# A cross-attention and mixture-of-experts kernel: how router logits are turned and added, and which engine normalises the first tile of a pair

## What is computed

```python
def xattn(q, k, v, mask, Wq, Wk, Wv, bq, bk, bv):
    qp = relu(q @ Wq + bq); kp = relu(k @ Wk + bk); vp = relu(v @ Wv + bv)
    logits = relu(qp @ kp.T) / sqrt(512) + mask
    return relu(logits @ vp)
def ffn(x, gate_w, Wu, Wv, Wo):
    topv, topi = top_k(x @ gate_w, 2)
    w = softmax(topv)
    Y = (silu(x @ Wu[e]) * (x @ Wv[e])) @ Wo[e]      # for each expert e
    return sum over the 2 chosen experts of w * Y
x = x + xattn(layernorm(x), ctx, ctx, ...)
x = x + ffn(layernorm(x), ...)
```

## Time and profile before

| | us |
|---|---|
| median of 3 runs | 447.36 |
| lowest, highest | 447.08, 450.7 |
| the profiled execution | 448.53 |
| its span, first to last instruction | 446.8 |

### The profile page before, as it was taken

The page is one execution under the profiler, slowest core; times in us unless marked ns, Lnnn a source line. Parts: engine busy times, 40 slices in busy tenths (PEclk is TensorE's granted clock), DMA queues, the critical chain, the costliest instruction groups (busy, mean ns, idle before and its releaser), DMA issues.

```text
span 446.8 us, 10794 instructions
## 1 busy us (share of the span) xinstructions
PE 422.6 (95%) x3206; PEld 377.5 (84%) x3206; DVE 345.6 (77%) x1102; ACT 275.0 (62%) x602; POOL 187.1 (42%) x214
## 2 busy tenths in 40 slices
PE   8999999999999999979898899999999899999990
PEld 6588998888889988878787689999998799999980
DVE  1779899999999999998778877766667577666661
ACT  1677777877877778767575566676754344444430
POOL 2001245555556556653467523333331533333341
PEclk9999999999999999999999999999999999999997
DMA  8713235755555655535758598999547999999500
GB/s 291 239 61 95 93 107 180 256 187 175 192 192 191 189 176 169 188 118 174 280 190 294 175 299 262 325 331 331 162 114 225 328 364 333 346 301 274 211 2 0
DMA packets 51800, 94.06 MB, mean 211 GB/s; under 512 B 7585, under 2 KB 18337, under 8 KB 51745
## 3 DMA queue, kind: packets, MB, share of 16 engines
q1 hardware_dynamic: 40384, 59.28, 42.3%
q0 software_dynamic: 11360, 34.09, 20.0%
HBM read 52.04 MB, written 44.97 MB: 217 GB/s over the span
## 4 chain that ended last, share of the span: by engine, by line
PE 54%; DVE 23%; ACT 6%; issue 6%; DMA 4%; SPq 3%; POOL 1%; POOLq 0%; DVEq 0%; ACTq 0%
PE psQ L1292 9%; PE psQ L1294 9%; PE psQ L1293 9%; PE psT L1288 6%; DVE st L916 4%; DVE x L905 3%; PE psS L1292 2%; DVE qpT L805 2%; PE psO L1292 2%; PE psQ L1288 2%; PE psO L1294 2%; PE psO L1293 2%; PE psZ L1292 2%; PE psZ L1294 2%; PE psZ L1293 2%
## 5 line engine op out<-in xcount | busy, mean ns | idle before, releaser
L805 DVE TENSOR_TENSOR qT<-psT,qT 128x512 fp32r<-128x512 f32 x110 | 74.3, 689 | 33.8 <-ACT qT L613 33.5
L1292 PE MATMUL psQ<-wuv,qT 128*128 x312 | 95.0, 304 | 0.0
L1293 PE MATMUL psQ<-wuv,qT 128*128 x312 | 88.4, 283 | 0.0
L1294 PE MATMUL psQ<-wuv,qT 128*128 x312 | 88.1, 282 | 0.0
L541 POOL DMA_INDIRECT z_dram<-zb x64 | 71.0, 1109 | 31.5 <-issue 15.2
L1292 PE MATMUL psQ<-qT,wq 128*128 128x256 f32 x256 | 75.3, 294 | 0.0
L613 ACT ACTIVATE qT<-psT 128x512 fp32r<-128x512 f32 x110 | 63.6, 594 | 18.0 <-PE psT L1288 18.0
L1294 PE MATMUL psQ<-qT,wq 128*128 128x256 f32 x256 | 72.5, 283 | 0.0
L1293 PE MATMUL psQ<-qT,wq 128*128 128x256 f32 x256 | 72.5, 283 | 0.0
L1292 PEld LDWEIGHTS psQ<-wuv,qT 128*128 128x128 f32 x312 | 59.2, 190 | 4.4
L1293 PEld LDWEIGHTS psQ<-wuv,qT 128*128 128x128 f32 x312 | 59.5, 191 | 0.0
(11 more groups left out here) (225 smaller groups left out, 1056.5 us busy)
## 6 DMA issues: line engine op xcount, KB each, us to landing
wq<-z_dram SPq DMA_DIRECT2D x46, 264.0 KB, 4.0
xin<-in_x_dram SPq DMA_DIRECT2D x11, 512.0 KB, 3.6
z_dram<-spare SPq DMA_DIRECT2D x18, 264.0 KB, 3.6
qpT<-z_dram SPq DMA_DIRECT2D x18, 264.0 KB, 4.0
xn<-z_dram SPq DMA_DIRECT2D x14, 264.0 KB, 3.1
xin<-acc_dram SPq DMA_DIRECT2D x13, 256.0 KB, 4.4
zT_ctxT<-acc_dram SPq DMA_DIRECT2D x12, 256.0 KB, 4.6
zT_ctxT<-in_x_dram SPq DMA_DIRECT2D x5, 512.0 KB, 3.4
```

The source lines that it names most:

```text
L805: nc.vector.tensor_tensor(o, a, b, ALU.subtract).then_inc(s, 1)
L1292: pe.matmul(o, w[LO], a[HI], start=first, stop=False)
L1293: pe.matmul(o, w[HI], a[LO], start=False, stop=False)
L1294: return pe.matmul(o, w[HI], a[HI], start=False, stop=last)
```

## The change

Three things are done.

- `turn_logits` turns each 128x128 tile of `logT` with a plain transpose, and writes the result over `ps_log`. VectorE then adds the four strips with one `tensor_reduce` from PSUM into `logits` in SBUF (a new operation in `choose.values()`, with a wait of VectorE for it), and `max` and `max_index` read `logits`. `gates` gets a wait for that operation of the block before.
- `pick`, its making at the start and TensorE's wait for it are gone.
- `norm_x` is gone from VectorE, in the loop and at the start. ScalarE normalises tile 0 as it does tile 1, one directly before the other, and one semaphore counts both. At the start it is ScalarE that waits for the end of the products over the ones.

```diff
--- before.py
+++ after.py
@@ -164,7 +164,6 @@
         before = sb("before", [P, P], BF16)
         ones = sb("ones", [P, P], BF16)
         gw = sb("gw", [P, DC, STRIP])
-        pick = sb("pick", [P, E])
         bq_sb = sb("bq_sb", [P, DC])
         bk_sb = sb("bk_sb", [P, DC])
         st1 = sb("st1", [P, TPB, 6])
@@ -181,6 +180,7 @@
         euler = sb("euler", [P, TPB])
         warm = sb("warm", [P, 1])
         logT = sb("logT", [P, BT])
+        logits = sb("logits", [P, TPB, E])
         top_v = sb("top_v", [P, TPB, 8])
         top_i = sb("top_i", [P, TPB, 8], U32)
         iota_e = sb("iota_e", [P, TPB, K, E], U32)
@@ -229,7 +229,7 @@
         ps_sched = [psS, psG, psG, psG]
         ps_key = [psS, psG, psQ[0], psQ[1]]
         ps_log = psG[:, 0:BT]
-        ps_logit = psG[:, BT:BT + TPB * E].rearrange("p (t e) -> p t e", e=E)
+        ps_strips = psG[:, 0:BT].rearrange("p (t c s) -> p t s c", t=TPB, s=STRIP)[:, :, 0:E, :]
         ps_pos = psG[:, BT + 32:BT + 32 + TPB * K * E].rearrange("p (t k e) -> p t k e", k=K, e=E)
         ps_tot = psG[:, BT + 96:BT + 96 + K * E].rearrange("p (k e) -> p k e", e=E)
         psST = [psQ[i][:, 2 * R:2 * R + P] for i in range(2)]
@@ -256,8 +256,7 @@
         stats1 = sem("stats1")
         rstd1_ready = sem("rstd1_ready")
         nmr1_ready = sem("nmr1_ready")
-        xn0_ready = sem("xn0_ready")
-        xn1_ready = sem("xn1_ready")
+        xn_ready = sem("xn_ready")
         xn_turned = sem("xn_turned")
         qT_hi = sem("qT_hi")
         qT_lo = sem("qT_lo")
@@ -286,6 +285,7 @@
         gate_done = sem("gate_done")
         logT_ready = sem("logT_ready")
         logit_turned = sem("logit_turned")
+        folded = sem("folded")
         route = sem("route")
         egap_ready = sem("egap_ready")
         den_ready = sem("den_ready")
@@ -631,7 +631,7 @@
 
                 ge(act, nmr1_ready, b.n + 1)
                 nc.scalar.activation(xn[:, t, 0:D], x_of(b)[:, t, :], ACT.Identity, bias=nmr1[:, t:t + 1],
-                                     scale=rstd1[:, t:t + 1]).then_inc(xn1_ready, 1)
+                                     scale=rstd1[:, t:t + 1]).then_inc(xn_ready, 1)
 
             def turned_x(b, t):
                 ge(act, xn_turned, 2 * b.n + t + 1)
@@ -727,6 +727,7 @@
                 if not nxt.real:
                     nc.scalar.activation(warm[:, :], minus_half[:, 0:1], ACT.Silu).then_inc(warmed, 1)
                 else:
+                    norm1(nxt, 0)
                     norm1(nxt, 1)
                 queries(2)
                 queries(3)
@@ -742,6 +743,8 @@
                 if nxt.real:
                     expert_high(b)
 
+            act.wait_ge(ones_used, 1)
+            norm1(Step(0), 0)
             norm1(Step(0), 1)
             act.wait_ge(w_loaded["bk"], 16)
             for m in (2, 3, 0, 1):
@@ -810,9 +813,7 @@
             nc.vector.tensor_copy(base[:, :, :], base_i[:, :, :]).then_inc(conv_ready, 1)
             nc.vector.tensor_copy(tile_s[:, :], tile_i[:, :]).then_inc(conv_ready, 1)
             nc.vector.tensor_copy(tok_f[:, :], tok_i[:, :]).then_inc(conv_ready, 1)
-            nc.vector.tensor_reduce(pick[:, :], ident[:, :].rearrange("p (c s) -> p s c", s=STRIP)[:, 0:E, :], AX.X,
-                                    ALU.add).then_inc(conv_ready, 1)
-            dve.wait_ge(conv_ready, 5)
+            dve.wait_ge(conv_ready, 4)
 
             key_rows = [lg[:, :], tl[:, :], tq[:, 0, :], tq[:, 1, :]]
 
@@ -950,13 +951,15 @@
 
                 def values(self):
                     ge(dve, logit_turned, self.b.n + 1)
+                    nc.vector.tensor_reduce(logits[:, :, :], ps_strips, AX.X, ALU.add).then_inc(folded, 1)
+                    ge(dve, folded, self.b.n + 1)
                     for t in range(TPB):
-                        nc.vector.max(top_v[:, t, :], ps_logit[:, t, :]).then_inc(route, 1)
+                        nc.vector.max(top_v[:, t, :], logits[:, t, :]).then_inc(route, 1)
 
                 def indices(self):
                     ge(dve, route, self.n + 2)
                     for t in range(TPB):
-                        nc.vector.max_index(top_i[:, t, :], top_v[:, t, :], ps_logit[:, t, :]).then_inc(route, 1)
+                        nc.vector.max_index(top_i[:, t, :], top_v[:, t, :], logits[:, t, :]).then_inc(route, 1)
 
                 def gaps(self):
                     ge(dve, egap_ready, self.b.n)
@@ -1061,10 +1064,6 @@
 
             def norm1_of(b):
                 return Norm(b, lambda t: x_of(b)[:, t, :], st1, mv1, ve1, nmr1, rstd1, stats1, rstd1_ready, nmr1_ready)
-
-            def norm_x(b):
-                nc.vector.tensor_scalar(xn[:, 0, 0:D], x_of(b)[:, 0, :], mv1[:, 0, 0:1], rstd1[:, 0:1],
-                                        ALU.subtract, ALU.mult).then_inc(xn0_ready, 1)
 
             def turned_x(b, t):
                 ge(dve, qT_hi, 2 * b.n + t + 1)
@@ -1130,7 +1129,6 @@
                     add_attention(prv, 1)
                 if nxt.real:
                     norm1.shift()
-                    norm_x(nxt)
                 if third.real:
                     put.ranks()
                     put.picked()
@@ -1176,8 +1174,6 @@
             norm1.moments(1)
             norm1.variance()
             norm1.shift()
-            dve.wait_ge(ones_used, 1)
-            norm_x(first)
             for c in range(DC):
                 dve.wait_ge(wq_hi, c + 1)
                 sub(wq[:, LO, c, :], wq_raw[:, c, :], wq[:, HI, c, :], wq_ready)
@@ -1373,7 +1369,7 @@
             def turn_x(b):
                 ge(pe, zT_ready, 2 * (b.n - 2))
                 for t in range(TPB):
-                    ge(pe, (xn0_ready, xn1_ready)[t], b.n + 1)
+                    ge(pe, xn_ready, 2 * b.n + t + 1)
                     for c in range(DC):
                         ins = turn(psT[t][:, c * P:(c + 1) * P], xn[:, t, c * P:(c + 1) * P])
                     ins.then_inc(xn_turned, 1)
@@ -1382,6 +1378,7 @@
                 if b.n == 0:
                     pe.wait_ge(w_loaded["small"], 32)
                 ge(pe, zT_ready, 2 * b.n + 2)
+                ge(pe, folded, b.n)
                 ge(pe, place, PLACE_STEPS * (b.n - 1) + 3)
                 for c in range(DC):
                     ins = pe.matmul(ps_log[c * STRIP:(c + 1) * STRIP, :], gw[:, c, :], zT[:, c, :], start=True, stop=True,
@@ -1400,10 +1397,8 @@
 
             def turn_logits(b):
                 ge(pe, logT_ready, b.n + 1)
-                if b.n == 0:
-                    pe.wait_ge(conv_ready, 5)
                 for t in range(TPB):
-                    ins = pe.matmul(ps_logit[:, t, :], logT[:, t * P:(t + 1) * P], pick[:, :], start=True, stop=True)
+                    ins = turn(ps_log[:, t * P:(t + 1) * P], logT[:, t * P:(t + 1) * P])
                 ins.then_inc(logit_turned, 1)
 
             def turn_sched(g):
```

## The result

The changed kernel takes 450.23 us (median of 6 runs, 449.35 to 451.85), the kernel before beside it 447.59 (6 runs): a ratio of 1.0056, 95% interval 1.0032 to 1.0079. It is 0.6% slower. The profiled execution took 450.61 us around a span of 448.9, 2.1 us more than before.

A forecast was written before the change was run, and what follows sets the result against it. VectorE looked like the bound, with ScalarE only 0.39 us ahead at low(2). Start 2.16, loop 0.36, fold 0.27, less 0.12 for a turned logit, gave +2.67 us: 450.0 us, range 446.4 to 452.0.

The forecast's parts named there:

- ScalarE's margin: Steady block, at low(2): ScalarE is only 0.39 us ahead of VectorE, so VectorE's saved 0.46 becomes waiting; block 11.88 us.
- ScalarE's price arrives in each block: Rival, steady blocks: the fold delays the shift, low(2) comes some 0.4 us late per block; 454.5 us, chance 0.13.
- The bound named for no saving on TensorE: Steady loop: if the transposes save nothing, 12 blocks are 0.12 us longer each, +1.4 us.
- TensorE's saving: Turning the logits, steady block: two transposes take 0.22 us where the products take 0.34, saving 0.12 us on the chain.
- Room for a gain: Steady block, ahead of scores: TensorE waits 0.53 to 0.60 us for VectorE, leaving room if nothing else arrives then.
- VectorE is the bound, and its relief arrives: Rival, steady blocks: low(2) comes earlier with VectorE, each block 0.46 us shorter; 444.1 us, or 441.9; chance 0.12.
- The cover of the shift: Steady block, tile 0's norm on ScalarE: its shift ends at 7.77, the norm starts at 7.90, leaving 0.13 us cover.
- The first blocks: Start, block 0 and block 1: ScalarE's second norm costs 0.72 us each, together 2.16 us.
- The start hides it: Rival, start: TensorE's slow first products cover the first norm and more; 448.6 or 447.8 us, chance 0.15.
- The fold: VectorE's sum of strips: 0.27 us with its wait, hidden in steady blocks, +0.27 us in the last block.
- The -0.12 for a turned logit ahead of an expert tile: TensorE, among the expert tiles: one of the last turned logits is ahead of a tile, saving 0.12 us.

The follow-up runs named there:

- kernel 6: The changed kernel with the fold done twice, one after the other; timed once at 452.69 us, steady block 11.959 us.
- kernel 3: The kernel before with only the norm of tile 0 moved to ScalarE, products with pick kept; ratio 1.0093 to the kernel before, steady block 11.979 us.
- kernel 5: The changed kernel with tile 0 normalised by VectorE for block 0 and by no engine later; 443.99 us, ratio 0.9908 to the kernel before.
- kernel 8: The changed kernel with VectorE normalising tile 0 in blocks 0 to 2, POOL's root first, tile 1's norm after query group 2; 444.67 us, ratio 0.9932.
- kernel 7: The changed kernel with POOL's root for the next block's norm ahead of its exponential; timed once at 449.5 us, steady block 11.747 us.
- kernel 2: The kernel before with transposes and fold alone, norm_x staying on VectorE; ratio 1.0000 to the kernel before, steady block 11.884 us.
- kernel 4: The changed kernel, but VectorE normalises tile 0 in blocks 0 to 2; ratio 1.0012 to the kernel before (0.9970 to 1.0054).
- kernel 9: The changed kernel again, unchanged, profiled and timed in a later series; 450.65 us, ratio 1.0071 to the kernel before.
- kernel 11: The kernel before with only the norm of tile 1 moved behind query group 2; 448.36 us, ratio 1.0008, steady block 11.879 us.
- kernel 12: Kernel 8 with the products by pick instead of transposes, and without the fold; 448.02 us, ratio 0.9998 to the kernel before, block 11.878 us.
- kernel 1: The changed kernel with one tiny ScalarE activation ahead of its waits at the start; ratio 1.0025 to the kernel before (0.9988 to 1.0061).
- kernel 10: The changed kernel with one tiny ScalarE activation ahead of its waits at the start, beside kernel 9; 450.10 us, ratio 1.0046.

## Why the prediction was right, and where it was not

**ScalarE's margin, the step that decided.** Right. VectorE's 0.46 us turned into a wait for ScalarE: 0.29 in the block shown, up to 0.4 elsewhere. Counted from `scores` (112.25), the z copies start at 6.83 (forecast 6.93), the norms at 7.85 (7.90), the ReLU at 9.28 (9.34), its copy at 9.76 (9.85), `low(2)` at 10.21 (10.31), and 1.58 (1.57) later `scores` again: 11.79 where I said 11.88. "ScalarE's price arrives in each block" did not happen: kernel 6 shows that even a second fold brings only 0.145. The bound named for no saving on TensorE, 12 blocks 0.12 longer, would make a block 12.00; kernel 3 has that case and takes 11.98.

**TensorE's saving.** Mis-sized: 0.22 instead of 0.12. I had counted the products and left out what they do to the next one. That is the 0.10 by which the z copies come earlier, and most of the miss in the loop: I charged +0.36 us and the loop gave about 0.5 back.

**Room for a gain.** The step "TensorE waits 0.53 to 0.60 us a block for VectorE ahead of `scores`" was misread. It is the wait of the weight load, which shows 0.51 and 0.52 in kernels 5 and 8 too, where TensorE's products never pause. The real room was 0.02 to 0.09. So the rival "VectorE is the bound, and its relief arrives" was overpriced at 0.46 a block: by these readings relief alone could not give 0.1, since TensorE stood right behind; no run has the relief without the transposes. It fell for more reasons than the one I gave.

**The cover of the shift.** I named VectorE's queue as what brings the shift. It is POOL's root, by 0.15 us in the block shown. The price is small (kernel 7: 0.067 a block). In kernel 2 it is 0.15, and with the fold on VectorE it cancels the whole benefit of TensorE's 0.22.

**The first blocks.** The second norm cost 0.70 at the start, 0.69 up to the first `scores` and 0.63 in block 0 to 1, against 0.72 each; the next distance gave 0.16 back. "The start hides it" is out, by these rows and by kernel 4.

**The table load.** Missed altogether, +1.35 us in the trace. The change list said that ScalarE gets a wait at its start; I asked what waits behind it, not what the program had placed ahead of the first function. This term stood at nothing in the sum. The Trainium skill ("ScalarE: Activation LUTs", What ACT_TABLE_LOAD costs) gives 1283 ns for the load and about 2.66 us with the draining of the engine, for a switch to another set. The trace agrees with the first (1.28) and shows no more than 1.35 in all; at the second load, at 206.15 us between two functions, it is 1.29 from the load's start to the next function's.

**The fold.** 0.21 us of work and 0.24 from start to start, forecast 0.27. In the last block it is on the chain, and cheaper than the +0.27 forecast: from the last `scores` to the attention product that waits for `logits_low` it was 3.64 us and is 3.76, so +0.12 (3.76 in kernel 9 too). The -0.12 for a turned logit ahead of an expert tile can't be read off, for the rest of the kernel moves by 0.8 us between two executions of one program. The wait of `gates` for it costs nothing.

**The total.** Forecast 450.0, measured 450.23; between the medians +2.67 against +2.64. It agrees so well because misses cancel, and that is luck: +1.35 of table load not seen, against 0.85 charged too much in the loop, 0.30 in the first blocks, 0.17 won in the last distance of `scores` and 0.09 at the end (the +0.15 of fold and transpose against the +0.06 of the table). That is 1.35 less 1.41, so +2.61 of span without the earlier input. Without the table load in the kernel, the same sum would have been 1.4 us too high.

**Four queues.** What the runs leave is a loop with four queues within 0.1 to 0.2 us of each other. The chain over VectorE sets 11.855 before the change; POOL with VectorE 11.88 if only TensorE is relieved (kernel 2); ScalarE 11.98 if only the norm is moved (kernel 3); TensorE with `pick` 11.88 when the norm of tile 1 comes late (kernels 11 and 12), of which 0.07 is its wait for that norm; its own pace with `pick` is some 11.80, an estimate from kernel 5's 11.576 and the 0.227. Two of them moved give 11.81 (the changed kernel), with POOL's root 11.75 (kernel 7), with ScalarE's order as well 11.65 (kernel 8).

Open: the single long block of kernel 4, and why ScalarE's table load lands behind the second wait. It does so in all five kernels that were profiled with two waits ahead of the first function (3, 6, 7, 9 and the changed one), and in none of the seven with one (before, 2, 4, 5, 8, 11 and 12) or the two with a small function first (1 and 10). The five also share the rest of that edit, the wait for the ones and the norm of tile 0 as first function, and no run parts these from the number of waits.

## What to carry to other kernels

Before a gain is counted from relieving the engine that seems to end last, write down for each other queue, TensorE's products and the small operations of GpSimd included, when it would be ready; where they are 0.1 us apart, an edit to one is worth nothing and three edits together may be worth what none is. Read TensorE's room from the starts of its products, not from the wait shown at a weight load. And when a wait is added ahead of ScalarE's first function, look where its table load goes.

## What the runs showed that was not expected

- ScalarE's table load of 1.28 us runs at 0.79 to 0.80 us in the kernels with one wait ahead of the first function, and behind the late wait, at 11.79 to 12.71 us, in those with two.
- A product of 256 columns behind fp32 products of 8 columns takes 0.22 us of the chain, and 0.12 behind two 128x128 fp32 transposes.
- A weight load can show 0.5 us of waiting for its operand in a stream of products without a pause.
- A norm of tile 1 that ends only after the transposes of tile 0 have begun costs TensorE 0.07 us a block (0.94 for eight transposes, not 0.87; kernels 8, 11 and 12).
- Two ScalarE norms of 128x512 in a row take 1.52 us, 0.70 to 0.72 apart, where one alone takes 0.81.
